# Cross-attention steps on TensorE: the weighted sums of the step just gone move between the two halves of a step's scores

## The chip, the cores and the metric

The kernel runs on one core of a Trainium2 chip. The metric is the device time of one execution in microseconds (us), as the median of three runs. The profile is one further execution of the same program; its own time stands beside its span.

## The reference, cut to what matters

The block takes x (2 batches of 256 query tokens, 256 wide) and a context of 4096 tokens per batch. It does a cross-attention with 16 heads of size 16, then a retention layer, then a layer of 8 experts, each with a layer norm in front and a residual behind. The change lies in the cross-attention:

```python
scores = jnp.einsum('bhqd,bhkd->bhqk', q, k) * scale
scores = jnp.where(mask, jnp.asarray(-jnp.inf, scores.dtype), scores)
weights = jax.nn.softmax(scores, axis=-1)
attn = jnp.einsum('bhqk,bhkd->bhqd', weights, v)
```

The mask hides all but the last keys, so that one window of 7 blocks of 128 keys is worked through.

## The kernel before, in words

The work is written out by hand, engine by engine, in one order each. The engines meet only at semaphores, and an instruction that waits holds back all that is written behind it on its engine.

**Stages and steps.** The 16 heads and 2 batches make 8 stages of 4 heads (`G = 4`) each, and a stage has 7 blocks of keys (`KB = 7`). A step is one block of keys in one stage, so there are `NU = 56` steps, n = 0 to 55; step n belongs to stage n // 7 and to key block n % 7. Below, "place 0" to "place 6" is n % 7.

**One step** in `steps` of TensorE has up to five pieces:

- `scores(c, n, 0)` and `scores(c, n, 1)`, the two halves of the scores (L724): two heads each, two matmuls of 99x128 by 99x256 in bf16. Each half has its own bank of PSUM. It waits until ScalarE has taken the exponential of the same half of the step before (`prob_ready` of at least n' - 1, with n' = 2n + half), because it overwrites that bank. At place 0 a third matmul of 512 columns adds the mask (L728).
- `max_tile`, a piece of the search for the row maxima of the next stage (L678, L683, L678: 448, 128 and 448 columns). VectorE reduces it in L1461. Steps 0, 1 and 2 and the steps at place 3 up to step 38 have two of them, the others up to step 44 have one, steps 45 to 55 have none. The first stands between the two halves of the scores, a second one behind them.
- `weighted(c, n - 1)`, the weighted sums of the step before (L740): 4 heads side by side in the array, each 32 columns wide, in fp32, which the trace shows as 8 matmuls of 256 columns. It waits for both exponentials of step n - 1 (`prob_ready` of 2(n - 1) + 2). At place 1, where the step before was the first of a stage, it also waits for `outT_ready`: ScalarE must have copied the sums of the stage before out of the bank that it starts to fill.
- at places 1 and 4, small transposes of the outputs (L707) and of the maxima (L699); at steps 5, 11 and 18 a block of keys or values for later (`LATER`), 8 or 16 fp32 matmuls; at steps 46 and 49 transposes and the output projection of the first batch (L791, L811).

**ScalarE** runs, in its own order, for each step: the exponential of the first half and of the second (`exps`, L1147, 128x512 each), then the copy of keys or values if the step has one, at place 0 the copy `outputs_out` of the stage's sums (L1136), at place 4 the copy of the maxima. After step 47 come four copies for the projection (L1185, L1176).

Below, S0(n) and S1(n) are the two halves of the scores of step n, T its piece of the maxima, W(n) the weighted sums over the probabilities of step n, and exp0(n), exp1(n) the two exponentials.

Of the kernel before, what the change touches and what calls it, by code (L numbers as in the profile page):

```python
# [17 lines left out]
NB = 2  # L18
# [46 lines left out]
NU = STAGES * KB  # L65
NVP = 4
# [116 lines left out]
def build(nc, a):  # L183
    with ExitStack() as ctx:
# [147 lines left out]
        def settle(eng):  # L332

            eng.sem_inc(s["settled"], 1)
# [241 lines left out]
        def _(pe):  # L576
# [31 lines left out]
            def take_pair(c, kind, n):  # L608
                at = c.ring_at[kind, n]
                if at >= 2:  # L610
                    if c.loop:
                        settle(pe)
                    pe.wait_ge(*release(c, *c.ring[at - 2]))
                return c.pair(kind, n)
# [41 lines left out]
            def max_tile(c, m):  # L656

                st, i = divmod(m, TILES)
                b, g = divmod(st, NG)
                qt, j = divmod(i, G)  # L660
                if i == 0:
                    pe.wait_ge(s["q_stacked1" if g >= 2 else "q_stacked0b" if b else "q_stacked0"], 96)
                    pe.wait_ge(*c.at(f"k_stacked{2 * b + g // 2}", 96))
                    if c.loop:
                        settle(pe)
                if m == 0:
                    pe.wait_ge(s["ident_ready"], 16 + 1)
                    pe.wait_ge(s["q_taken"], KIN)
                    if c.loop:
                        pe.wait_ge(*c.at("hide_ready", 1))  # L670
                    else:
                        pe.wait_ge(s["hide_first"], 2)
                pair = take_pair(c, "m", m)
                h = G * g + j
                for half_ in range(2):
                    out = bank[:, pair + half_, 0:HC]
                    hides = c.loop or half_ == 0
                    mm = pe.matmul(out, qstack[0:MROW, h, b, qt * P:(qt + 1) * P], kstack[0:MROW, b, h, half_ * HC:(half_ + 1) * HC],  # L678
                                   start=True, stop=not hides, skip_group_check=True)
                    if c.loop:  # L680
                        mm = pe.matmul(out, identb[:, :], hide_q[:, qt, half_ * HC:(half_ + 1) * HC], start=False, stop=True, skip_group_check=True)
                    elif half_ == 0:
                        pe.matmul(out[:, 0:P], identb[:, :], hide_q0[:, qt, :], start=False, stop=True, skip_group_check=True)  # L683
                mm.then_inc(c["max_ready"], 1)
# [10 lines left out]
            def turn_rows(c, st):  # L695
                pe.wait_ge(*c.at("max_cut", st + 1))
                take_last_bank(c, "rows", st)
                for qt in range(QT):
                    mm = pe.transpose(xbank_b[0:3 * G, qt * P:(qt + 1) * P],  # L699
                                      mpart[:, st % 2, qt, :, :].rearrange("p c h -> p (c h)"), identb[:, :])  # L700
                mm.then_inc(c["rows_turned"], 1)

            def turn_outputs(c, st):
                pe.wait_ge(*c.at("outT_ready", st + 1))
                take_last_bank(c, "out", st)
                for qt in range(QT):
                    mm = pe.transpose(bank[:, XB, qt * P:(qt + 1) * P], outT[:, st % 2, qt * P:(qt + 1) * P], ident[:, :])  # L707
                mm.then_inc(c["out_turned"], 1)

            def scores(c, u, jj):  # L710
                st, kt = divmod(u, KB)
                b, g = divmod(st, NG)
                n = 2 * u + jj
                if n >= 2:
                    pe.wait_ge(*c.at("prob_ready", n - 1))
                elif c.loop:
                    pe.wait_ge(*c.at("v_evac", NVP))
                else:
                    pe.wait_ge(*c.at("k_taken", 3))
                out = bank[:, S0 + jj, :]  # L720
                hides = c.loop or kt == 0
                for hh in range(2):
                    h = G * g + 2 * jj + hh
                    mm = pe.matmul(out[:, hh * NQ:(hh + 1) * NQ], kstack[0:KROWS, b, h, kt * P:(kt + 1) * P], qstack[0:KROWS, h, b, :],  # L724
                                   start=(hh == 0 or not hides), stop=not hides, skip_group_check=True)
                if hides:
                    hidden = hide_k[:, kt, :] if c.loop else hide_k0[:, :]
                    mm = pe.matmul(out, identb[:, :], hidden.unsqueeze(1).to_broadcast([P, 2, NQ]),  # L728
                                   start=False, stop=True, skip_group_check=True)
                mm.then_inc(c["score_ready"], 1)  # L730

            def weighted(c, u):
                st, kt = divmod(u, KB)
                b, g = divmod(st, NG)
                if kt == 0 and st:
                    pe.wait_ge(*c.at("outT_ready", st))
                pe.wait_ge(*c.at("prob_ready", 2 * u + 2))
                for j in range(G):
                    e = (G * g + j) * E1
                    mm = pe.matmul(bank[32 * j:32 * j + PADV, OB, 0:NQ], vals[:, b, kt, e:e + PADV],  # L740
                                   prob[:, (2 * u + j // 2) % PROBS, (j % 2) * NQ:(j % 2 + 1) * NQ], start=(kt == 0), stop=(kt == KB - 1),
                                   tile_position=(0, 32 * j), skip_group_check=True)
                mm.then_inc(c["prob_used"], 1)

            def steps(c):
                pe.wait_ge(s["ones_loaded"], 16)
                for n in range(NU):
                    st, kt = divmod(n, KB)
                    tiles = list(TILES_AT[n])
                    if kt == 0:  # L750
                        pe.wait_ge(*c.at(f"mrows_loaded{st % 2}", 16 * (st // 2 + 1)))
                        if c.loop:
                            settle(pe)
                    scores(c, n, 0)
                    if tiles:
                        max_tile(c, tiles.pop(0))
                    scores(c, n, 1)
                    for m in tiles:
                        max_tile(c, m)
                    if n in LATER and not c.loop:  # L760
                        kind, i = LATER[n]
                        (keys if kind == "k" else later_values)(c, i)
                    if n:
                        if n == NU // NB + 1:
                            pe.wait_ge(*c.at("v_evac", NVP + 2))
                        weighted(c, n - 1)
                    if n in OUT_AT:
                        turn_outputs(c, OUT_AT[n])
                    if n in ROWS_AT:
                        turn_rows(c, ROWS_AT[n])  # L770
                    if n == AT_TURNED and not c.loop:
                        pe.wait_ge(*c.at("max_read", NT))
                        turn_at(0)
                        turn_at(1)
                    if n == AT_TURNED + 3 and not c.loop:
                        attention_out(0)
                        attention_out(1)
                weighted(c, NU - 1)
                turn_outputs(c, STAGES - 1)
# [27 lines left out]
            def attention_out(t):  # L807
                pe.wait_ge(s["wo_loaded"], 32)
                taken("at", t)
                for c in range(KIN):  # L810
                    mm = pe.matmul(bank[:, AT_BANKS[t], 0:D], xnT[:, c, t * P:(t + 1) * P], wo[:, c, :], start=(c == 0), stop=(c == KIN - 1))  # L811
                mm.then_inc(s["o_ready"], 1)

            def turn_at(t):
                pe.wait_ge(s["at_ready"], t + 1)
                turn("at", t, bank[:, turn_bank("at", t), :], at_tok[:, t, :], KIN)
# [207 lines left out]
            with pe.If(fast > 0):  # L1024
                steps(only)
                tail_of_all()
# [726 lines left out]
```

## Time and profile before

| what | value |
|---|---|
| median of 3 runs | 249.11 us (248.33 to 250.49) |
| the profiled execution's own time | 248.6 us |
| its span, first to last instruction | 246.8 us |
| TensorE busy | 228.2 us, 92% of the span |
| VectorE busy | 149.2 us, 60% |
| ScalarE busy | 111.6 us, 45% |
| steps 0 to 55, from the first L724 to the last L740 | 43.15 to 150.6 us of the span |
| granted clock of TensorE | 1.00 in every stretch |

The busy time of an engine is the time in which at least one of its instructions was in flight. A row such as "PE bank L724 10%" of the chain names the line whose instruction the end of the program hung on for that share of the span. The span has three parts: loads and projections up to about 43 us, the 56 steps up to about 151 us, and the second layer and the experts up to 246.8 us. The change touches the middle one.

### The profile page before, as it was taken

The numbers are of one execution on the slowest core, as the hardware profiler recorded it, in microseconds if no ns is written. First come the engines' busy times: TensorE is split into PE (matmuls) and PEld (weight loads), VectorE is DVE, ScalarE is ACT, GpSimd is POOL, SyncE is SP. The second block draws the span as 40 slices with busy tenths as digits, with TensorE's granted clock in tenths as the row PEclk, the third lists the DMA queues.
The fourth block names the chain that finished last, engine by engine and source line by source line (L and its number), as shares of the span: only waits on it lengthen the run. The fifth ranks groups of instructions, "written<-read, shape, count | busy, mean of one in ns | idle before, by whom it ended". The sixth has DMA issues, their size and how long they took to land.

```text
span 246.8 us, 3909 instructions
## 1 busy us (share of the span) xinstructions
PE 228.2 (92%) x1454; PEld 127.7 (52%) x1454; DVE 149.2 (60%) x340; ACT 111.6 (45%) x234; POOL 25.0 (10%) x28
## 2 busy tenths in 40 slices
PE   7979998999999999999999898989898889899892
PEld 7846684444565645454544433534746763635340
DVE  1656494893836748787876063485457538586682
ACT  2143463565747567777777784323144041201000
POOL 7002340805400400000000000000000000000000
PEclk9999999999999999999999999999999999999999
DMA  6659996909008800460000000000000000000000
GB/s 198 201 128 222 341 228 119 335 6 227 1 0 203 230 4 0 114 230 1 3 4 3 1 3 0 0 1 0 3 0 0 0 1 3 1 0 21 23 28 25
DMA packets 14541, 17.94 MB, mean 73 GB/s; under 512 B 2468, under 2 KB 13620, under 8 KB 14516
## 3 DMA queue, kind: packets, MB, share of 16 engines
q1 hardware_dynamic: 13220, 17.28, 25.5%
q10 hardware_dynamic: 1295, 0.34, 0.9%
q8 instruction: 14, 0.23, 0.4%
q14 instruction: 12, 0.09, 0.1%
HBM read 9.79 MB, written 0.52 MB: 42 GB/s over the span
## 4 chain that ended last, share of the span: by engine, by line
PE 70%; DVE 18%; ACT 5%; issue 3%; DMA 2%; SPq 0%; POOL 0%; DVEq 0%; ACTq 0%; POOLq 0%
PE bank L740 10%; PE bank L724 9%; PE bank L923 8%; PE bank L678 8%; DVE cneg L1461 7%; PE bank L830 6%; PE bank L579 4%; PE bank L633 4%; PE bank L640 4%; PE bank L903 3%; PE bank L791 3%; DMA qstack<-xbo 2%; ACT prob L1147 2%; PE bank L811 1%; PE bank L728 1%
## 5 line engine op out<-in xcount | busy, mean ns | idle before, releaser
L1461 DVE TENSOR_REDUCE cneg<-bank 128x1 f32<-128x896 f32 x64 | 68.2, 1088 | 33.1 <-PE bank L678 33.0
L1147 ACT ACTIVATE prob<-bank 128x512 f32<-128x512 f32 x112 | 65.6, 598 | 25.5 <-PE bank L724 17.0
L724 PE MATMUL bank<-qstack,kstack 99*128 99x256 bf16 x224 | 42.3, 274 | 1.7 <-ACT k_full L1100 0.8
L678 PE MATMUL bank<-kstack,qstack 96*128 96x448 bf16 x128 | 38.6, 354 | 0.8 <-DMA qstack<-xbo 0.4
L740 PE MATMUL bank<-prob,vals 128*32 128x256 f32 x448 | 35.8, 391 | 0.4 <-ACT prob L1147 0.4
L724 PEld LDWEIGHTS bank<-qstack,kstack 99*128 99x128 bf16 x224 | 17.5, 97 | 25.5 <-issue 12.1
L830 PE MATMUL bank<-w_late,xnT 128*128 128x512 f32 x48 | 22.0, 595 | 0.3 <-ACT xnT L1176 0.3
L678 PEld LDWEIGHTS bank<-kstack,qstack 96*128 96x128 bf16 x128 | 12.5, 98 | 9.6 <-DVE cneg L1461 1.7
L923 PE MATMUL bank<-ctxT,xnT 128*128 128x512 f32 x32 | 17.1, 616 | 0.3 <-DVE x_in L1641 0.3
L1641 DVE SCALAR_TENSOR_TENSOR x_in<-bank,nwts,x_in 128x256 f32<-128x256 f32 x32 | 15.5, 484 | 2.5 <-PE bank L923 1.4
L923 PE MATMUL bank<-kpart,xnT 128*128 128x512 f32 x32 | 16.3, 592 | 0.0
L740 PEld LDWEIGHTS bank<-prob,vals 128*32 128x32 f32 x448 | 8.8, 108 | 14.1 <-issue 11.1
L579 PE MATMUL bank<-ones 128*128 128x128 f32 x98 | 13.5, 297 | 1.5 <-POOL ones L481 1.4
L683 PE MATMUL bank<-hide_q,identb 128*128 128x128 bf16 x64 | 14.0, 219 | 0.0
L579 PEld LDWEIGHTS bank<-ones 128*128 128x128 f32 x98 | 13.1, 211 | 1.8 <-POOL ones L481 1.4
L640 PE MATMUL bank<-wv,ctxT 128*128 128x256 f32 x56 | 13.1, 383 | 0.2
L830 PEld LDWEIGHTS bank<-w_late,xnT 128*128 128x128 f32 x48 | 8.5, 190 | 8.2 <-issue 7.7
L633 PE MATMUL bank<-ctxT,wk 128*128 128x448 f32 x32 | 12.8, 542 | 0.0
L1176 ACT ACTIVATE xnT<-bank 128x256 f32<-128x256 f32 x8 | 3.0, 384 | 19.7 <-PE bank L791 19.7
L640 PEld LDWEIGHTS bank<-wv,ctxT 128*128 128x128 f32 x56 | 10.5, 190 | 2.3 <-DVE cneg L1461 0.7
L1500 DVE COPY acc<-bank 128x136 f32<-128x136 f32 x8 | 2.4, 299 | 13.0 <-PE bank L707 12.6
L923 PEld LDWEIGHTS bank<-kpart,xnT 128*128 128x128 f32 x32 | 6.1, 190 | 7.7 <-issue 7.7
(142 smaller groups left out, 260.4 us busy)
## 6 DMA issues: line engine op xcount, KB each, us to landing
kstack<-kpart SPq DMA_DIRECT2D x24, 224.0 KB, 4.5
w_late<-in_w_ret SPq DMA_DIRECT2D x1, 1536.0 KB
mask_all<-in_mask SPq DMA_DIRECT2D x2, 512.0 KB, 6.0
ctxT<-in_w_exp SPq DMA_DIRECT2D x1, 1024.0 KB
kpart<-in_w_exp SPq DMA_DIRECT2D x1, 1024.0 KB
ctxT<-in_ctxT SPq DMA_DIRECT2D x2, 448.0 KB, 6.2
ctxT<-in_ctxT SPq DMA_DIRECT2D x1, 896.0 KB, 9.4
qstack<-acc SPq DMA_DIRECT2D x6, 128.0 KB, 6.4
```

The lines of the kernel that those rows point to most:

```text
L579: pe.matmul(bank[:, where, 0:P], ones[:, :], ones[:, :], start=True, stop=True)
L633: mm = pe.matmul(bank[:, banks + h, 0:HC], wk[:, i, f * P:(f + 1) * P], ctxT[:, b, i, h * HC:(h + 1) * HC], start=(i == 0), stop=(i == KIN ...
L640: mm = pe.matmul(out[:, (k - blocks[0]) * D:(k - blocks[0] + 1) * D], ctxT[:, b, i, k * P:(k + 1) * P], wv[:, i, :], start=(i == 0), stop= ...
L678: mm = pe.matmul(out, qstack[0:MROW, h, b, qt * P:(qt + 1) * P], kstack[0:MROW, b, h, half_ * HC:(half_ + 1) * HC], start=True, stop=not h ...
L683: pe.matmul(out[:, 0:P], identb[:, :], hide_q0[:, qt, :], start=False, stop=True, skip_group_check=True)
L724: mm = pe.matmul(out[:, hh * NQ:(hh + 1) * NQ], kstack[0:KROWS, b, h, kt * P:(kt + 1) * P], qstack[0:KROWS, h, b, :], start=(hh == 0 or no ...
L740: mm = pe.matmul(bank[32 * j:32 * j + PADV, OB, 0:NQ], vals[:, b, kt, e:e + PADV], prob[:, (2 * u + j // 2) % PROBS, (j % 2) * NQ:(j % 2 + ...
L830: mm = pe.matmul(bank[:, 2 + m, :], xnT[:, c, t * P:(t + 1) * P], w_ret[:, c, m * 512:(m + 1) * 512], start=(c == 0), stop=(c == KIN - 1))
L923: mm = pe.matmul(bank[:, PAIR_BANKS[m % 4], :], xnT[:, c, t * P:(t + 1) * P], w_exp[c][:, 2 * pr:2 * pr + 2, :], start=(c == 0), stop=(c = ...
L1147: act.activation(prob[:, n % PROBS, :], bank[:, S0 + jj, :], ACT.Exp).then_inc(c["prob_ready"], 1)
L1461: dve.tensor_reduce(cneg[:, st % 2, i:i + 1], bank[:, pair:pair + 2, 0:HC], AXXY, ALU.max, negate=True).then_inc(c["max_read"], 1)
L1641: dve.scalar_tensor_tensor(x_in[:, t, :], src, nwts[:, t, e:e + 1], x_in[:, t, :], ALU.mult, ALU.add).then_inc(s["pair_read"], 1)
```

## The change

Four lines move within `steps` of TensorE: `weighted(c, n - 1)` with its one wait for the values of the second batch stood behind both halves of the scores and behind `LATER`, and stands now between the two halves, behind the step's first `max_tile`. No instruction is added or taken away, and no other engine's list changes.

```diff
                     scores(c, n, 0)
                     if tiles:
                         max_tile(c, tiles.pop(0))
+                    if n:
+                        if n == NU // NB + 1:
+                            pe.wait_ge(*c.at("v_evac", NVP + 2))
+                        weighted(c, n - 1)
                     scores(c, n, 1)
                     for m in tiles:
                         max_tile(c, m)
                     if n in LATER and not c.loop:
                         kind, i = LATER[n]
                         (keys if kind == "k" else later_values)(c, i)
-                    if n:
-                        if n == NU // NB + 1:
-                            pe.wait_ge(*c.at("v_evac", NVP + 2))
-                        weighted(c, n - 1)
                     if n in OUT_AT:
                         turn_outputs(c, OUT_AT[n])
```

TensorE's list at a step of place 1 (scores, maxima, weighted sums, transposes of the outputs), before:

```order
L724 MATMUL bank<-qstack,kstack 128x256 [waits prob_ready]
L724 MATMUL bank<-qstack,kstack 128x256
L678 MATMUL bank<-kstack,qstack 128x448 [waits max_read]
L683 MATMUL bank<-hide_q,identb 128x128
L678 MATMUL bank<-kstack,qstack 128x448
L724 MATMUL bank<-qstack,kstack 128x256 [waits prob_ready]
L724 MATMUL bank<-qstack,kstack 128x256
L740 MATMUL bank<-prob,vals 32x256 [waits prob_ready,outT_ready]
L740 MATMUL bank<-prob,vals 32x256 x3
L707 MATMUL bank<-ident,outT 128x128 [waits mrows_ready,outT_ready]
L707 MATMUL bank<-ident,outT 128x128
```

And the same step now:

```order
L724 MATMUL bank<-qstack,kstack 128x256 [waits prob_ready]
L724 MATMUL bank<-qstack,kstack 128x256
L678 MATMUL bank<-kstack,qstack 128x448 [waits max_read]
L683 MATMUL bank<-hide_q,identb 128x128
L678 MATMUL bank<-kstack,qstack 128x448
L740 MATMUL bank<-prob,vals 32x256 [waits prob_ready,outT_ready]
L740 MATMUL bank<-prob,vals 32x256 x3
L724 MATMUL bank<-qstack,kstack 128x256 [waits prob_ready]
L724 MATMUL bank<-qstack,kstack 128x256
L707 MATMUL bank<-ident,outT 128x128 [waits mrows_ready,outT_ready]
L707 MATMUL bank<-ident,outT 128x128
```

The weighted sums, with their waits for the exponentials and for the copied-out sums, went ahead of the second half of the scores.

TensorE's list over one step without maxima (of steps 51 to 55), before:

```order
L724 MATMUL bank<-qstack,kstack 128x256 [waits prob_ready]
L724 MATMUL bank<-qstack,kstack 128x256
L724 MATMUL bank<-qstack,kstack 128x256 [waits prob_ready]
L724 MATMUL bank<-qstack,kstack 128x256
L740 MATMUL bank<-prob,vals 32x256 [waits prob_ready]
L740 MATMUL bank<-prob,vals 32x256 x3
```

And now:

```order
L724 MATMUL bank<-qstack,kstack 128x256 [waits prob_ready]
L724 MATMUL bank<-qstack,kstack 128x256
L740 MATMUL bank<-prob,vals 32x256 [waits prob_ready]
L740 MATMUL bank<-prob,vals 32x256 x3
L724 MATMUL bank<-qstack,kstack 128x256 [waits prob_ready]
L724 MATMUL bank<-qstack,kstack 128x256
```

The two halves of one step, which stood side by side, have the weighted sums between them, and the second half stands side by side with the first half of the next step.

## Rows read from the trace of the kernel before

**Rows 1.** The page, part 1: busy time, share of the span and instructions by engine.
```profile
PE 228.2 (92%) x1454; PEld 127.7 (52%) x1454; DVE 149.2 (60%) x340; ACT 111.6 (45%) x234; POOL 25.0 (10%) x28
```

**Rows 2.** The page, part 5: count, busy us, mean ns | idle before, releaser.
```profile
L1147 ACT ACTIVATE prob<-bank 128x512 f32<-128x512 f32 x112 | 65.6, 598 | 25.5 <-PE bank L724 17.0
```

**Rows 3.** Busy time by stretch: PE, PEld, DVE, ACT, POOL, clock, DMA; the steps without maxima.
```profile
132.48:149.93 17.45, 16.16 (x155) 7.10 (x151) 5.92 (x25) 13.69 (x29) 0.00 (x0) 1.00 0.01 1
```

**Rows 4.** Timeline of PE, steps 34 to 37: start, us, what [idle before].
```profile
101.31 0.39 PE L724 MATMUL bank<-qstack,kstack 99*128 99x256 bf16 x2
101.54 0.35 PE L678 MATMUL bank<-kstack,qstack 96*128 96x448 bf16 x1
...
101.80 0.35 PE L678 MATMUL bank<-kstack,qstack 96*128 96x448 bf16 x1
101.99 0.38 PE L724 MATMUL bank<-qstack,kstack 99*128 99x256 bf16 x2
102.30 0.64 PE L740 MATMUL bank<-prob,vals 128*32 128x256 f32 x8
102.87 0.39 PE L724 MATMUL bank<-qstack,kstack 99*128 99x256 bf16 x2
103.10 0.38 PE L728 MATMUL bank<-hide_k,identb 128*128 128x512 bf16 x1
103.32 0.35 PE L678 MATMUL bank<-kstack,qstack 96*128 96x448 bf16 x1
...
103.98 0.38 PE L728 MATMUL bank<-hide_k,identb 128*128 128x512 bf16 x1
104.29 0.64 PE L740 MATMUL bank<-prob,vals 128*32 128x256 f32 x8
...
106.42 0.44 PE L707 MATMUL bank<-ident,outT 128*128 128x128 f32 x2
106.69 0.38 PE L724 MATMUL bank<-qstack,kstack 99*128 99x256 bf16 x2
```

**Rows 5.** Timeline of ACT, steps 34 and 35.
```profile
101.74 1.26 ACT L1147 ACTIVATE prob<-bank 128x512 f32<-128x512 f32 x2 [0.30 <-PE bank L724]
...
104.40 0.60 ACT L1147 ACTIVATE prob<-bank 128x512 f32<-128x512 f32 x1 [0.28 <-PE bank L728]
105.00 0.37 ACT L1136 COPY outT<-bank 128x256 f32<-128x256 f32 x1
```

**Rows 6.** Timeline of PE, ends of steps 38 (two tiles) and 39 (transposed maxima).
```profile
109.38 0.35 PE L678 MATMUL bank<-kstack,qstack 96*128 96x448 bf16 x1
109.66 0.64 PE L740 MATMUL bank<-prob,vals 128*32 128x256 f32 x8
...
111.22 0.64 PE L740 MATMUL bank<-prob,vals 128*32 128x256 f32 x8
111.67 0.28 PE L699 MATMUL bank<-identb,mpart 128*12 128x128 bf16 x2
111.88 0.39 PE L724 MATMUL bank<-qstack,kstack 99*128 99x256 bf16 x2
```

**Rows 7.** Timeline of PEld, the weight load behind the same L740.
```profile
111.46 0.30 PEld L699 LDWEIGHTS bank<-identb,mpart 128*12 128x12 bf16 x2
```

**Rows 8.** Timeline of PE in steps 4 and 44 to 55: W(43), W(50), W(55).
```profile
52.19 0.36 PE L678 MATMUL bank<-kstack,qstack 96*128 96x448 bf16 x1 [0.18 <-DVE cneg L1461]
...
131.91 0.64 PE L740 MATMUL bank<-prob,vals 128*32 128x256 f32 x8
...
143.97 0.64 PE L740 MATMUL bank<-prob,vals 128*32 128x256 f32 x8
...
149.93 0.64 PE L740 MATMUL bank<-prob,vals 128*32 128x256 f32 x8 [0.39 <-ACT prob L1147]
```

**Rows 9.** Timeline of ACT, the exponentials of step 55.
```profile
148.79 1.09 ACT L1147 ACTIVATE prob<-bank 128x512 f32<-128x512 f32 x2 [0.26 <-PE bank L724]
```

## The prediction

> **What bounds the kernel now.** I read the shares of the engines first: TensorE is busy for 92% of the span, no other engine for more than 60% [rows 1]. So what TensorE does or waits for between 43 and 151 us is what counts. Next the timeline of TensorE over whole steps [rows 4]. An ordinary step with one tile, step 34, runs from 101.31 to 102.87: 1.56 us, in which TensorE never stands idle. The starts lie S0 to T 0.23, T to its last matmul 0.26, that to S1 0.19, S1 to W 0.31, W to the next S0 0.57 us. ScalarE works 1.26 us of it, then waits 0.30 us for TensorE [rows 5]. In these steps TensorE is the bound and the exponentials have slack. In the steps without maxima it is the other way: from W(50) at 143.97 to W(55) at 149.93 [rows 8] a step takes 5.96 / 5 = 1.19 us (the last of them 1.03), about the 1.09 us of two exponentials and their handover [rows 9], and TensorE is idle for 17.45 - 16.16 = 1.3 us of that stretch [rows 3].
>
> **Which chain the change makes.** S1(n) must wait for exp1(n-1), whose bank it overwrites; W(n-1) waits for the same exponential. Before, W stood behind S1, so the circle was S1, exp1, S1: an exponential starts 0.43 us after its scores (101.31 to 101.74) [rows 4, 5], takes 0.60 us [rows 2], and TensorE goes on 0.05 us after its end (148.79 + 1.09 = 149.88, W at 149.93) [rows 8, 9]: 1.08 us, and W was done under the exponentials. Now W lies in the circle, S1, exp1, W, S1. From W to a following full-width load is 0.57 us [rows 4], so the circle takes 1.08 + 0.57 = **1.65 us**. It is compared with the time TensorE needs anyway.
>
> **Ordinary steps with one tile.** In the new order TensorE's own distances are S1 to S0 0.23 (as S0 to T), S0 to T 0.23, T to its last matmul 0.26, that to W 0.28 (109.38 to 109.66) [rows 6], W to S1 0.57: 1.57 us, the same work. From S1 to W are 1.00 us, where the exponential needs 1.08. So W waits 0.08 us. This counts only where nothing else stands between S1 and W: the W of places 3 and 6 in steps 10 to 41, 10 steps, **0.8 us**. At places 2, 4 and 5 transposes or a second tile stand between and cover it, at place 0 the mask matmul.
>
> **Place 1, the change of stage.** W there also waits for the copy of the old sums, which ScalarE does behind exp1 of place 0. Counted from the mask matmul L728 of S1 (103.98): exp1 at 0.42 (104.40), its end at 1.02, the copy's 0.37 us to 1.39 [rows 4, 5], 0.05 for TensorE to see it: 1.44 us. TensorE itself would be there after 0.22 (L728 to the next bf16 matmul, 103.10 to 103.32) + 0.23 + 0.26 + 0.28 = 0.99 us. Wait 0.45 us, at steps 8, 15, 22, 29, 36 and 43: **2.7 us**. Before, S1 stood ahead of this W and covered the copy.
>
> **Transposes that lose their place behind W.** L699 has weights of 12 columns; its load starts 0.24 us after W (111.46) [rows 7] and W to S0 with it takes 0.66 us [rows 6], 0.09 more than without. Behind S1 it costs its own 0.21 (111.67 to 111.88). That is 0.12 us at 6 steps, **0.7 us**. L707 costs 0.27 us (106.42 to 106.69) [rows 4] and now stands between bf16 matmuls; going from bf16 to fp32 cost 0.28 against 0.19 us above, so 0.09 us at 6 steps, **0.5 us**. The three blocks of LATER do the same: **0.2 us**. Both are bounded by nothing and twice that.
>
> **Steps 0 to 6.** Here TensorE waits for VectorE's maxima (0.18 us in front of a tile at 52.19) [rows 8]. A tile that comes somewhat later is still ahead of VectorE. I take **0.2 us**, between nothing and 0.4.
>
> **Steps 44 to 55.** From W(50) to W(55) five circles: 5 x 1.65 = 8.25 us instead of 5.96, **2.3 us**. From W(43) to W(50), 12.06 us before [rows 8], I lay the same durations out again: W(44), W(45), W(47) and W(50) each come 0.3 us later and W(49) too, as their S1 stood bare before them. W(46) loses 0.1 and W(48) gains 0.2, since ScalarE's four copies after step 47 held the scores back before as well, and the output projection in step 49 covers exp1(49). Together **1.4 us**, between 0.8 and 3.2 (seven times 1.65 - 1.19).
>
> **What costs nothing.** The second layer starts when the last sums are out, so all of this is passed on to the end. The loads for it and the maxima are not nearer to being late than before: rows of maxima are written at place 4, three steps before they are read, and these steps get longer, not shorter. SyncE's and GpSimd's lists do not change.
>
> **Sum.** 0.8 + 2.7 + 0.7 + 0.5 + 0.2 + 0.2 + 2.3 + 1.4 = 8.8 us. The profiled execution took 248.6 us, so 257.4; against the median of 249.1 it is 257.9. I predict **257.5 us**, 3.4% slower.
>
> **Where a rule of the chip would give something else.** The row shows: behind W, a load of 128 columns starts only with the next matmul, 0.57 us on, and one of 12 columns after 0.24 us [rows 4, 7]. If the weights of S1 came in under W, its matmul would start after 0.45 us (111.22 to 111.67) [rows 6], and with the way into W at 0.19 instead of 0.28 us TensorE would gain about what place 1 loses: the circle is 1.53 us, the steps with tiles come out even, and only steps 44 to 55 lose, some 2.5 us: 251.6 us. The Trainium skill's page "TensorE: Matmul & The Clock Gate", section "Step-by-step: what each phase is for", has a rule that would lead there: the queue pulls weight loads ahead of matmuls in flight while matmuls keep their order. By that rule, rival A below; the trace shows it for the 12 columns alone, so I go by the row. The second half of the rule, that matmuls keep their order, is what my circle needs; no row here shows a matmul overtake.
>
> **Rivals.**
> - **A, the weights of S1 load under W:** 251.6 us. For it: L699. Against it: every L724 and L707 behind an L740 starts 0.57 us after it. 5%.
> - **B, no change, because S1 overtakes a waiting W.** S1's own wait is met at the same moment as W's, so a TensorE that took S1 first would be back at the old order: 249.1 us, or up to 1.3 us less if W filled the idle time of [rows 3]. It decides from the first W that waits, at place 1. Against it: at 149.93 and 52.19 the engine simply stands. 4%, and 2% that it ends over 1% faster.
> - **C, each wait costs more than 0.05 us.** If a resumed TensorE loses up to 0.2 us, as a weight load cannot go ahead of a wait, 27 waits (10 + 6 + 11) add 4 us: 261.4 us. 8%.
> - **D, the clock falls.** In the steps without maxima TensorE would be idle a third of each circle. At the lower level of 1.2 GHz W and S1 would take twice as long and 11 circles gain 0.5 us each: 263 us. The granted clock was 1.00 there [rows 3]. 3%.
>
> That leaves 78% for the forecast, itself 254.5 to 260.5 by the bounds above.
>
> **Numbers.** 1% (2.5 us) is about what a measurement can tell here. Slower by over 1%: forecast, C, D, and most of A: 92%. Same: B and the rest of A, 6%. Faster: 2%. The range that holds it 8 times in 10 is 253.5 to 261.0.
>
> **What would show it.** In the profile after, ScalarE's L1147 no longer comes in pairs of 1.26 us but singly; L740 waits for L1147 in about 20 steps and for the copy L1136 in six, by 0.4 to 0.5 us; in steps 51 to 55 L740 repeats every 1.65 us; seven steps in the middle take 0.8 us longer together. It is wrong if W to S1 is under 0.5 us, or if L740 at place 1 does not wait.

## The result and the profile after

The changed kernel takes 257.04 us (median of 4 runs, 255.74 to 257.76) against 249.31 us before: a ratio of 1.030, 95% interval 1.024 to 1.037, **slower by 7.7 us**. The forecast was 257.5 us. The profiled execution took 255.74 us with a span of 253.9 us, 7.1 more than before.

A correction first: the rows called steps 34 to 37 and 38 to 39 in the groups 4 to 6 above are those of steps 27 to 30 and 31 to 32, one stage earlier (and so is "step 34" of the prediction, which is step 27). The places in the stage, and so all numbers, are the same.

The page of the changed kernel, part 1 and the lines of part 5 that answer to [rows 1, 2]:

```profile
PE 230.4 (91%) x1454; PEld 128.9 (51%) x1454; DVE 149.7 (59%) x340; ACT 107.6 (42%) x234; POOL 25.0 (10%) x28
...
L1147 ACT ACTIVATE prob<-bank 128x512 f32<-128x512 f32 x112 | 63.6, 596 | 37.6 <-PE bank L724 29.7
L740 PE MATMUL bank<-prob,vals 128*32 128x256 f32 x448 | 35.8, 391 | 6.2 <-ACT prob L1147 4.2
```

TensorE's list is as long as before and its busy time grew by 2.2 us only, where the span grew by 7.1: most of what grew is idle time. ScalarE's idle time in front of an exponential grew from 25.5 to 37.6 us, and L740 now has 6.2 us of idle time ahead of it. Each waits for the other, which is what a closed circle looks like on a page.

TensorE over places 0 and 1 of the same stage as in [rows 4], after the change (start, us, instruction [idle before]):

```profile
104.52 0.61 PE L724 MATMUL bank<-qstack,kstack 99*128 99x256 bf16 x4
104.97 0.38 PE L728 MATMUL bank<-hide_k,identb 128*128 128x512 bf16 x1
...
105.72 0.64 PE L740 MATMUL bank<-prob,vals 128*32 128x256 f32 x8
106.29 0.39 PE L724 MATMUL bank<-qstack,kstack 99*128 99x256 bf16 x2
106.52 0.38 PE L728 MATMUL bank<-hide_k,identb 128*128 128x512 bf16 x1
106.74 0.38 PE L724 MATMUL bank<-qstack,kstack 99*128 99x256 bf16 x2
...
107.21 0.35 PE L678 MATMUL bank<-kstack,qstack 96*128 96x448 bf16 x1
107.90 0.64 PE L740 MATMUL bank<-prob,vals 128*32 128x256 f32 x8 [0.33 <-ACT outT L1136]
108.47 0.39 PE L724 MATMUL bank<-qstack,kstack 99*128 99x256 bf16 x2
108.70 0.38 PE L707 MATMUL bank<-ident,outT 128*128 128x128 f32 x2
108.92 0.38 PE L724 MATMUL bank<-qstack,kstack 99*128 99x256 bf16 x2
```

ScalarE at the same time:

```profile
106.94 0.60 ACT L1147 ACTIVATE prob<-bank 128x512 f32<-128x512 f32 x1 [0.91 <-PE bank L728]
107.43 0.37 ACT L1136 COPY outT<-bank 128x256 f32<-128x256 f32 x1
107.69 0.62 ACT L1147 ACTIVATE prob<-bank 128x512 f32<-128x512 f32 x1
```

W at place 1 starts 0.69 us after the tile's last matmul (107.21 to 107.90) where 0.28 would do: a wait of 0.41 us for the copy, which ended at 107.80. At the five other changes of stage with a tile the same distance is 0.64 us, a wait of 0.36. Behind W the scores S1 come after 0.57 us, as before.

The steps without a tile, TensorE's last two W and the exponentials between them, answering to [rows 8, 9]:

```profile
155.66 0.64 PE L740 MATMUL bank<-prob,vals 128*32 128x256 f32 x8 [0.47 <-ACT prob L1147]
156.23 0.39 PE L724 MATMUL bank<-qstack,kstack 99*128 99x256 bf16 x2
157.31 0.64 PE L740 MATMUL bank<-prob,vals 128*32 128x256 f32 x8 [0.69 <-ACT prob L1147]
```

```profile
155.01 1.08 ACT L1147 ACTIVATE prob<-bank 128x512 f32<-128x512 f32 x2 [0.56 <-PE bank L724]
156.66 0.60 ACT L1147 ACTIVATE prob<-bank 128x512 f32<-128x512 f32 x1 [0.56 <-PE bank L724]
```

155.66 to 157.31 is 1.65 us. The parts can be read off: 0.57 to S1 (156.23), 0.43 to its exponential (156.66), 0.60 for that, 0.05 to W. The stretch of these steps, as in [rows 3]:

```profile
136.14:157.31 21.17, 16.32 (x153) 7.34 (x151) 5.62 (x25) 14.28 (x29) 0.00 (x0) 1.00 0.00 1
```

TensorE is idle for 4.9 of 21.2 us, before for 1.3 of 17.5. How much later each W starts than before, from the two timelines:

| W of step | 5 | 28 | 35 | 42 | 43 | 50 | 55 | end of span |
|---|---|---|---|---|---|---|---|---|
| later by us | 0.15 | 2.05 | 2.77 | 3.49 | 3.44 | 5.09 | 7.38 | 7.1 |

The first scores already started 0.16 us later (43.31 against 43.15). A stage with tiles costs 0.72 us, the last five steps alone 2.3 us.

### The profile page after: what moved, and what is told of

The parts are those of the page before. It is cut to its first block, busy times and chain, and to the rows that moved or that the text cites. A ratio compares the mean times of both kernels' runs of the same rounds, so it can differ in the third digit from the quotient of the medians.

```text
span 253.9 us, 3909 instructions
## 1 busy us (share of the span) xinstructions
PE 230.4 (91%) x1454; PEld 128.9 (51%) x1454; DVE 149.7 (59%) x340; ACT 107.6 (42%) x234; POOL 25.0 (10%) x28
## 4 chain that ended last, share of the span: by engine, by line
PE 75%; DVE 14%; ACT 6%; issue 4%; POOL 0%; ACTq 0%; DVEq 0%; POOLq 0%
PE bank L740 13%; PE bank L724 10%; PE bank L923 8%; PE bank L678 7%; PE bank L830 6%; PE bank L633 5%; PE bank L640 5%; PE bank L579 4%; DVE cneg L1461 4%; PE bank L903 3%; PE bank L791 3%; ACT prob L1147 2%; PE bank L597 1%; PE bank L811 1%; PE bank L728 1%
## 5 line engine op out<-in xcount | busy, mean ns | idle before, releaser
L1147 ACT ACTIVATE prob<-bank 128x512 f32<-128x512 f32 x112 | 63.6, 596 | 37.6 <-PE bank L724 29.7
L740 PE MATMUL bank<-prob,vals 128*32 128x256 f32 x448 | 35.8, 391 | 6.2 <-ACT prob L1147 4.2
L724 PE MATMUL bank<-qstack,kstack 99*128 99x256 bf16 x224 | 39.8, 275 | 1.5 <-ACT k_full L1100 0.8
L724 PEld LDWEIGHTS bank<-qstack,kstack 99*128 99x128 bf16 x224 | 16.6, 97 | 29.0 <-ACT prob L1147 19.2
L740 PEld LDWEIGHTS bank<-prob,vals 128*32 128x32 f32 x448 | 8.9, 108 | 21.1 <-ACT prob L1147 14.4
L579 PE MATMUL bank<-ones 128*128 128x128 f32 x98 | 14.1, 306 | 1.4 <-POOL ones L481 1.4
L579 PEld LDWEIGHTS bank<-ones 128*128 128x128 f32 x98 | 13.7, 220 | 1.8 <-POOL ones L481 1.4
```

The source lines that it names most:

```text
L579: pe.matmul(bank[:, where, 0:P], ones[:, :], ones[:, :], start=True, stop=True)
L1147: act.activation(prob[:, n % PROBS, :], bank[:, S0 + jj, :], ACT.Exp).then_inc(c["prob_ready"], 1)
```

## The experiments

The theory is the circle: W's 0.57 us lie between an exponential and the scores whose exponential comes next, and the copy of the old sums lies in it at place 1. The rival is that the order of the pieces, or stopping and restarting, costs by itself. The kernel before measured 249.3 us beside the changed kernel, 248.9 us beside four of the kernels below and 248.6 us beside the other four, and the changed kernel was timed in the first set alone. So "less than the change" is best read from the loss against the kernel before in the same set, and from the traces. These agree closely where the lists do: up to the first scores of step 45 the trace with the wait alone repeats that of the kernel before within 0.02 us, counted from the first scores.

| kernel | against before, medians of its set | first scores | end of W(55) | apart | more than before |
|---|---|---|---|---|---|
| before | | 43.15 | 150.57 | 107.42 | |
| the change | 7.7 | 43.31 | 157.95 | 114.64 | 7.2 |
| the wait alone | 0.1 | 43.45 | 151.14 | 107.69 | 0.3 |
| place 1 in the old order | 7.0 | 42.99 | 156.95 | 113.96 | 6.5 |
| the copy early | 6.3 | 43.00 | 156.58 | 113.58 | 6.2 |
| last eleven steps in the old order | 4.1 | 43.18 | 154.51 | 111.33 | 3.9 |
| sums one step older | 0.7 | 43.95 | 152.28 | 108.33 | 0.9 |
| that, and L699 behind W | 0.0 | 43.17 | 150.59 | 107.42 | 0.0 |

**The wait alone.** In the kernel before:

```diff
                         max_tile(c, tiles.pop(0))
+                    if n:
+                        pe.wait_ge(*c.at("prob_ready", 2 * n))
                     scores(c, n, 1)
```

> The kernel before, with the moved wait for both exponentials of step n-1 (the one of W(n-1)) put between the halves of the scores, and W itself left where it was. Theory (circle): S1(n) waits for the same exponential anyway, so the wait costs nothing and the time is that of before, 249.3 us, within 1 us. Rival (the wait is what costs, each stop and restart of TensorE or the weight load it holds back): most of the 7.7 us appears, 254 us or more.

Measured 249.05 us, ratio 1.002 (0.999 to 1.004). The wait costs next to nothing: S1 waits for that exponential in any case. In the trace it adds nothing up to the first scores of step 45, and 0.3 us in the steps without a tile behind them; why it is not quite free there stays open. What costs is W between the wait and S1.

**W back at its old place at place 1 alone.** In the changed kernel the condition of the new place became `if n and n % KB != 1`, and that of the old one, behind `LATER`, its opposite.

> The changed kernel, with W at its old place in the eight steps of place 1 alone. Theory (at place 1 W waits for the copied-out sums, 0.41 us in each of the six steps with a tile): 2.5 us less than the changed kernel, 254.5 us, and no wait of L740 for L1136 but the last. Rival (the order of the pieces costs evenly in every step, 7.7 us / 56 = 0.14 us each): 8 x 0.14 = 1.1 us less, 255.9 us.

Measured 255.88 us, 7.0 us above the kernel before where the change is 7.7 above: 0.7 us less, and 0.7 in the traces too. That is far from the 2.5 of the theory and nearer the rival's 1.1; its trace says why:

```profile
106.19 0.38 PE L728 MATMUL bank<-hide_k,identb 128*128 128x512 bf16 x1
106.42 0.38 PE L724 MATMUL bank<-qstack,kstack 99*128 99x256 bf16 x2
...
106.89 0.35 PE L678 MATMUL bank<-kstack,qstack 96*128 96x448 bf16 x1
107.26 0.39 PE L724 MATMUL bank<-qstack,kstack 99*128 99x256 bf16 x2
107.59 0.64 PE L740 MATMUL bank<-prob,vals 128*32 128x256 f32 x8
...
108.43 0.38 PE L724 MATMUL bank<-qstack,kstack 99*128 99x256 bf16 x2
```

With W early at place 0 and late at place 1 there is no W between the two S1, and S1 waits for the exponential itself: 0.37 us after the tile (106.89 to 107.26) instead of 0.19. The step takes 2.01 us (106.42 to 108.43), with the change 2.18 (106.74 to 108.92), with the old order throughout 1.83 (104.86, the start of step 29, to 106.69). So of W's wait of 0.41 us, 0.17 is saved, 0.18 comes back in front of S1, and the transposes behind W cost 0.05 more again (0.27 against 0.22). In the five other stages the step is 0.12 us shorter than with the change. The expectation missed the wait that stood behind the one it removed. The run does not tell how much of the 0.41 is the copy's; the next one does.

**The copy ahead of the exponential.** The change on TensorE stays; on ScalarE:

```diff
                     exps(c, 2 * n)
+                    if n and n % KB == 0:
+                        outputs_out(c, n // KB - 1)
                     exps(c, 2 * n + 1)
 ...
-                    if n and n % KB == 0:
-                        outputs_out(c, n // KB - 1)
```

> The changed kernel, with one change on ScalarE: the copy of a finished stage's sums (L1136) stands between the two exponentials of place 0, no longer behind both. TensorE's order is that of the change. Theory (W at place 1 waits for the copy behind exp1; with the copy ahead of exp1 it waits for exp1 alone, 0.1 us instead of 0.41): 6 x 0.31 = 1.9 us less than the changed kernel, 255.1 us. Rival (what place 1 costs is the scores meeting bare, as e2_place1_back's 0.17 us a stage suggests, and the copy has little part in it): 256 to 257 us.

Measured 254.96 us, 6.3 us above the kernel before where the change is 7.7 above: 1.4 us less, and 1.1 in the traces. W at place 1 comes 0.46 us after the tile (here 106.40 to 106.86), so 0.18 us late, and no longer waits for the copy:

```profile
104.90 0.64 PE L740 MATMUL bank<-prob,vals 128*32 128x256 f32 x8
...
106.40 0.35 PE L678 MATMUL bank<-kstack,qstack 96*128 96x448 bf16 x1
106.86 0.64 PE L740 MATMUL bank<-prob,vals 128*32 128x256 f32 x8
```

```profile
105.61 0.37 ACT L1136 COPY outT<-bank 128x256 f32<-128x256 f32 x1 [0.39 <-PE bank L740]
106.12 1.08 ACT L1147 ACTIVATE prob<-bank 128x512 f32<-128x512 f32 x2
```

Moving a copy of 0.37 us on an engine that is 42% busy gives about 1.1 us, 0.17 us in each of five stages and 0.22 in this one. That the median, 254.96, lies on the 255.1 of the expectation is in part luck: the gain forecast was 1.9 us. The copy's part in place 1 is shown, and it is about half of the wait. Of the remaining 0.18 us the circle of the exponential explains about 0.1, as at places 3 and 6; the rest is that W starts 0.14 us behind the exponential's end here (106.12 + 0.60 = 106.72), not 0.05, which no run explains.

**The last eleven steps in the old order.** As above, with the condition `n < 45`.

> The changed kernel, with W at its old place in steps 45 to 55, those without a tile. Theory (the circle of 1.65 us exceeds what a step took before by 0.4 us only there): W(55) falls back from 7.4 us late to 3.7, so 253.3 us, and from W(50) to W(55) 5.96 us as before. Rival (even cost of 0.14 us a step): 11 x 0.14 = 1.5 us less, 255.5 us.

Measured 252.97 us, 4.1 us above the kernel before where the change is 7.7 above: 3.7 us less, 3.3 in the traces. W(50) to W(55) takes 5.95 us (147.92 to 153.87), the old value:

```profile
147.92 0.64 PE L740 MATMUL bank<-prob,vals 128*32 128x256 f32 x8
...
153.87 0.64 PE L740 MATMUL bank<-prob,vals 128*32 128x256 f32 x8 [0.39 <-ACT prob L1151]
```

Nearly half of the loss comes from a fifth of the steps, which an even cost of 0.14 us a step (1.5 us) does not give.

**The same order with older sums.** W between the halves is that of step n-2:

```diff
-                    if n:
-                        if n == NU // NB + 1:
+                    if n > 1:
+                        if n == NU // NB + 2:
                             pe.wait_ge(*c.at("v_evac", NVP + 2))
-                        weighted(c, n - 1)
+                        weighted(c, n - 2)
 ...
+                weighted(c, NU - 2)
                 weighted(c, NU - 1)
```

(`OUT_AT` one step later, and the copy between the two exponentials of place 1.)

> The order of the changed kernel, but the weighted sums between the halves of step n are those of step n-2 and not n-1 (W(54) and W(55) stand together at the end); the copy of a finished stage's sums goes between the two exponentials of place 1, and its transposes one step later. Same pieces in the same places on TensorE, but no W waits for the exponential just started. Theory (circle): the waits go, the steps without tiles take 1.11 us (0.31 + 0.57 + 0.23), below the 1.19 of before; what stays is 0.2 us at each L699 and less at the loads for later: 249 us, between 248 and 250. Rival (it is the order of the pieces, the switch of the array between wide and narrow weights twice a step and scores side by side across steps): 256 to 257 us.

Measured 249.59 us, ratio to the kernel before 1.004 (1.003 to 1.006): all but about 1 us of the loss is gone, and in the trace no idle time stands in front of an L740, though TensorE's pieces stand where the change put them (only the transposes L707 come a step later). So it is not their order. The step of the theory that was too hopeful is 1.11 us for a step without a tile; W(51) to W(53) (147.53, 148.86, 149.99) shows 1.33 and 1.13, no better than before.

```profile
147.53 0.64 PE L740 MATMUL bank<-prob,vals 128*32 128x256 f32 x8
148.10 0.83 PE L724 MATMUL bank<-qstack,kstack 99*128 99x256 bf16 x4
148.86 0.64 PE L740 MATMUL bank<-prob,vals 128*32 128x256 f32 x8
149.43 0.63 PE L724 MATMUL bank<-qstack,kstack 99*128 99x256 bf16 x4
149.99 0.64 PE L740 MATMUL bank<-prob,vals 128*32 128x256 f32 x8
```

**And the small transposes back behind W.** In addition to the last:

```diff
                         weighted(c, n - 2)
+                    if n in ROWS_AT:
+                        turn_rows(c, ROWS_AT[n])
                     scores(c, n, 1)
 ...
-                    if n in ROWS_AT:
-                        turn_rows(c, ROWS_AT[n])
```

> The lagging order of e5_lag, with the transposes of the maxima (L699, 12 columns of weights) moved from behind the second half of the scores to directly behind the weighted sums. Theory (a load of 12 columns goes in under W and a wide one does not, so L699 costs 0.09 us behind W and 0.30 between scores): 0.21 us less at seven steps, 1.5 us less than e5_lag, 248.1 us, and 0.5 to 1 us less than the kernel before. Rival (the place of L699 does not matter, its 0.30 us is what 128 columns and a change of type cost anywhere): 249.6 us as e5_lag.

Measured 248.66 us, 0.9 us less than the last, ratio to the kernel before 1.0005 (0.9985 to 1.0024). A wide load follows L699 as it did before: W 110.85, L699 111.30, S1 111.51, so 0.66 us from W to the scores. Without L699 it is 0.57; L699 costs 0.09 us there and 0.30 between scores.

```profile
110.85 0.64 PE L740 MATMUL bank<-prob,vals 128*32 128x256 f32 x8
111.30 0.27 PE L699 MATMUL bank<-identb,mpart 128*12 128x128 bf16 x2
111.51 0.61 PE L724 MATMUL bank<-qstack,kstack 99*128 99x256 bf16 x4
```

The place of L699 matters; the sum of 1.5 us was too large, since two of the seven steps hold a block of LATER as well: in the traces the gain is about 0.2 us in each of the other five, and about 0.1 lost in those two together. It only draws level with the kernel before; no experiment points to one that beats it.

**W half as long.** In the changed kernel and in the kernel before, W(50) to W(54) over 128 columns of 256, so that half of these sums is left out (one execution each, read from its trace):

```diff
+                cols = NQ // 2 if 50 <= u < NU - 1 else NQ
```

> The changed kernel with W(50) to W(54) cut to half their columns (128 of 256 queries; the other half of these sums is left out). Theory (W's length lies in the circle): each of the five circles is shorter by half of W's streaming, 0.57 us to about 0.36, so L740 repeats every 1.44 us instead of 1.65 and W(50) to W(55) is about 7.2 us instead of 8.25. Rival (stops and restarts of TensorE and of ScalarE make the 1.65, not W's length): it stays over 8.0 us.

> The kernel before with the same W(50) to W(54) cut to half their columns. Theory (there W is done under the exponentials and the exponentials are the bound): W(50) to W(55) stays 5.9 to 6.0 us, though five W are 0.2 us shorter each. Rival (TensorE's own work is the bound there too): 5 x 0.2 = 1 us less, 5.0 us.

In the changed kernel L740 repeats every 1.44 us (151.84 to 153.28) and W(50) to W(55) takes 7.18 us, as the circle gives:

```profile
151.84 0.43 PE L741 MATMUL bank<-prob,vals 128*32 128x128 f32 x8 [0.47 <-ACT prob L1148]
152.20 0.61 PE L724 MATMUL bank<-qstack,kstack 99*128 99x256 bf16 x4
153.28 0.42 PE L741 MATMUL bank<-prob,vals 128*32 128x128 f32 x8 [0.47 <-ACT prob L1148]
```

In the kernel before, W(50) to W(55) falls from 5.96 to 5.53 us (144.37 to 149.90), between the two expectations: the same cut gives 1.07 us in the changed kernel and 0.43 here. So the exponentials alone were not the bound of those steps; about 0.1 us of each was TensorE's.

## Why the prediction was right, point by point

- **The circle.** Right: 1.65 us forecast, 1.65 measured, with each of its four parts; shortening W shortens it one for one (0.57 to 0.36 us, 1.65 to 1.44), and making W older removes it. W(50) to W(55): 8.25 us forecast and measured.
- **W(43) to W(50).** 1.4 us forecast, 5.09 - 3.44 = 1.65 measured. From the first scores of step 44 to W(55) the two stretches lost 3.7 us, as forecast (2.3 + 1.4).
- **Places 3 and 6.** 0.08 us forecast in ten steps; the trace has it in nine, 0.9 us together: for the tile's last matmul to W 116.46 to 116.83, 0.37 instead of 0.28, so 0.09 us.

```profile
116.46 0.35 PE L678 MATMUL bank<-kstack,qstack 96*128 96x448 bf16 x1
...
116.83 0.64 PE L740 MATMUL bank<-prob,vals 128*32 128x256 f32 x8
```

- **Place 1.** The wait for the copy was there, mis-sized: 0.45 us forecast, 0.36 in five stages and 0.41 in one, so 2.2 us and not 2.7. The prediction let the copy start when the exponential's 0.60 us were over, as at 105.00 [rows 5]. But there the copy was held by its own W, which had started 0.71 us before (104.29); with the copy early it starts 0.71 us behind its W too (104.90, 105.61). After the change only the exponential stands before it, and it starts 0.49 us behind the exponential's start.
- **Transposes and LATER.** The term that was mis-sized most: 1.4 us forecast, about 0.2 measured up to step 44. L707 behind scores costs 0.22 us, 0.05 less than before, and not 0.09 more: the 0.09 us was taken from the way into W and is not a price of going to fp32. L699 costs more than I took: 0.53 us from S1 to S0 against 0.23, so 0.21 us more than before, not 0.12:

```profile
113.89 0.39 PE L724 MATMUL bank<-qstack,kstack 99*128 99x256 bf16 x2
114.21 0.28 PE L699 MATMUL bank<-identb,mpart 128*12 128x128 bf16 x2
114.42 0.39 PE L724 MATMUL bank<-qstack,kstack 99*128 99x256 bf16 x2
```

And the blocks of values in steps 11 and 18 gained, since the maxima that their bank waited for are read by the time that W has passed. Step 11 before (S1, values, W, L699, S0):

```profile
67.78 0.38 PE L724 MATMUL bank<-qstack,kstack 99*128 99x256 bf16 x2
68.25 3.72 PE L640 MATMUL bank<-wv,ctxT 128*128 128x256 f32 x16
71.90 0.64 PE L740 MATMUL bank<-prob,vals 128*32 128x256 f32 x8
```

And after (S1, values, L699):

```profile
69.22 0.39 PE L724 MATMUL bank<-qstack,kstack 99*128 99x256 bf16 x2
69.45 3.62 PE L640 MATMUL bank<-wv,ctxT 128*128 128x256 f32 x16
73.00 0.28 PE L699 MATMUL bank<-identb,mpart 128*12 128x128 bf16 x2
```

From S1 to the values 0.47 us before, 0.23 after. The steps before 44 lost 3.5 us (the first scores of step 44 start at 134.60 instead of 130.94, less the 0.16 of the start): 2.2 at place 1, 0.9 at places 3 and 6, 0.2 in steps 0 to 6 as forecast, and 0.2 that are left for transposes and LATER. The sum had 5.1.

- **The total.** 8.8 us forecast, 7.2 in the traces, and for the profiled execution 257.4 against 255.74 us. That 257.5 lies 0.5 us from the median of 257.04 is luck: the profiled execution is the fastest of four, and their median stands 1.3 us above it.
- **Rivals.** A: no weights of S1 came in under W, W to S1 stayed 0.57 us. The Trainium skill's page "TensorE: Matmul & The Clock Gate", section "Step-by-step: what each phase is for", lets the queue pull weight loads ahead of matmuls in flight where the row groups do not conflict or the load goes to the background weight buffer; the trace does not show it for the wide loads behind W. B: TensorE stood at each waiting W. C: a resumed TensorE lost 0.05 us in the steps without tiles and at five of the six changes of stage, 0.10 at the one shown (the copy's end 107.80, W 107.90), and the kernel with the wait alone lost 0.3 us in all. D: the granted clock was 1.00 in the stretch of these steps, 0.995 over the whole execution.
- **Signs.** L740 waits in 18 places for the exponential, where about 20 were forecast (the page puts idle time down to nine, since short waits hide behind matmuls still in flight), and in six for the copy. One sign did not come: the exponentials do not come singly. They come in pairs of 1.08 us, exp1 of a step and exp0 of the next (155.01), since S1(n) and S0(n+1) now stand side by side.

## What to carry to other kernels

Before moving a piece of work between two others on one engine, write down the circle through the other engine: what this engine gives, how long the other takes, what is taken back. A piece that is done while the other engine works costs little (cutting W to half gained 0.09 us a step in the old order and 0.21 in the circle); the same piece between taking back and giving again costs its full length in each turn (0.57 us), although no instruction and no wait was added. If it must stand there, let it work on older results; and look on the other engine for a short copy that stands in front of what is waited for.

## What was not expected of the hardware

- Two ScalarE instructions whose inputs are ready start 0.49 us apart though each is shown 0.60 us long (exponential 106.94, copy 107.43). A shown length is thus not the time for which an instruction holds back the next.
- Between wide bf16 matmuls, two fp32 transposes with 128 columns of weights cost 0.22 us and two bf16 ones with 12 columns 0.30 us, so it is not the change of type that costs. W too has narrow weights, and the way into it costs 0.28 us where 0.19 is usual. That points at the narrow loads, but it is not shown: no run varied the width alone.
